# A graph network's dense part and the norm behind it as one program of five groups, and look-ups in batches of four columns

## The reference

```python
    x = x + _L0_gnn_ref(_layernorm(x, axis=-1), src, dst, edge_weight, ...)
    x = x + _L0_ffn_ref(_layernorm(x, axis=-1)[None], ...)[0]
# in _L0_gnn_ref:
        new_x = jax.ops.segment_sum(gathered, rows, num_segments=N_NODES)
        out1 = new_x @ hamilton1
        mean = jnp.mean(out1, axis=0)
        var = jnp.mean(jnp.square(out1 - mean), axis=0)
        out1 = (out1 - mean) * jax.lax.rsqrt(var + BN_EPS) * gamma + beta
        out1 = jnp.tanh(out1)
        return out1 @ hamilton2
# in _L0_ffn_ref:
            h = (x_flat @ W_gat).reshape(M, HEADS, NUM_EXPERTS)
```

## Time and profile before

| | |
|---|---|
| median of 3 runs | 3285.32 us (3279.65 to 3296.63) |
| the profiled execution | 3290.92 us |
| its span in the trace | 3289.1 us |
| from the first addition of stage 1 to the last copy into `HG` | 1016.85 to 1189.28 us, 172.4 us |

### The profile page before, as it was taken

How to read it: one execution, slowest core, us unless ns; L and a number is a source line. 1 busy time by engine, 2 the same in 40 slices (tenths; PEclk the granted TensorE clock), 3 DMA queues, 4 the chain that set the end, 5 groups by cost and what they waited for, 6 DMA issues and landing times. The chain is left out here.

```text
span 3289.1 us, 50105 instructions
## 1 busy us (share of the span) xinstructions
PE 2310.9 (70%) x10737; PEld 1726.7 (52%) x10738; DVE 1916.3 (58%) x4697; ACT 839.4 (26%) x2016; POOL 1502.0 (46%) x1250
## 2 busy tenths in 40 slices
PE   3567787777753589999536677777777756229973
PEld 2456565555542367777413455555555534229961
DVE  3756777777674333333475477777777755324437
ACT  0112122212111322223111344444444411003320
POOL 0487888888870027770200455555455500240023
PEclk8667777778775869999657899899899977569985
DMA  6666777777775024220252555555455523422233
GB/s 223 139 98 113 114 126 117 126 115 127 125 103 163 1 89 129 64 58 33 66 160 79 163 155 156 143 144 151 135 153 146 142 71 129 149 69 70 70 117 93
DMA packets 264384, 380.36 MB, mean 116 GB/s; under 512 B 36635, under 2 KB 195251, under 8 KB 264115
## 3 DMA queue, kind: packets, MB, share of 16 engines
q0 software_dynamic: 108320, 187.88, 29.0%
q1 hardware_dynamic: 134579, 151.42, 14.9%
q10 hardware_dynamic: 21344, 39.59, 3.3%
HBM read 247.23 MB, written 131.54 MB: 115 GB/s over the span
## 5 line engine op out<-in xcount | busy, mean ns | idle before, releaser
L1113 POOL DMA_INDIRECT sum_tab<-Vs,spot x416 | 703.8, 1692 | 180.4 <-issue 99.0
L2276 POOL DMA_INDIRECT KV<-kv_tab,iS x448 | 446.4, 996 | 276.3 <-DVE msg L2376 128.2
L1019 PE MATMUL psV<-XN,Bs 128*128 x832 | 314.9, 486 | 158.6 <-issue 131.1
L1019 PEld LDWEIGHTS psV<-XN,Bs 128*128 128x128 f32 x832 | 155.4, 226 | 291.2 <-issue 284.4
L2440 PE MATMUL psQ<-Qs,hotT 128*128 x904 | 264.5, 443 | 21.1 <-issue 12.7
L2451 PE MATMUL psO<-msg,hot 128*128 128x264 f32 x896 | 241.9, 416 | 13.9 <-DVE msg L2376 7.5
L1088 ACT COPY Vs<-psV 128x512 f32<-128x512 f32 x208 | 121.7, 585 | 470.2 <-DMA sum_tab<-Vs,spot 381.7
L2440 PEld LDWEIGHTS psQ<-Qs,hotT 128*128 128x128 f32 x904 | 182.1, 218 | 88.8 <-issue 59.1
L1538 POOL DMA_INDIRECT ST<-h_tab,src x192 | 184.0, 958 | 58.5 <-issue 58.5
L2305 DVE TENSOR_TENSOR KV<-KV,psQ 128x1024 f32<-128x1024 f32 x112 | 136.8, 1221 | 126.5 <-issue 88.9
L2451 PEld LDWEIGHTS psO<-msg,hot 128*128 128x128 f32 x896 | 172.0, 202 | 59.7 <-issue 22.0
(11 more groups left out here) (538 smaller groups left out, 4300.7 us busy)
## 6 DMA issues: line engine op xcount, KB each, us to landing
kb<-key_rows SPq DMA_DIRECT2D x104, 256.0 KB, 3.9
sum_tab<-zeros ACTq DMA_DIRECT2D x52, 256.0 KB, 3.1
parts<-sum_tab SPq DMA_DIRECT2D x20, 640.0 KB, 6.8
ye_tab<-Ye SPq DMA_DIRECT2D x20, 640.0 KB, 3.5
Y<-ye_tab SPq DMA_DIRECT2D x20, 640.0 KB, 9.6
disp_tab<-AE ACTq DMA_DIRECT2D x10, 896.0 KB, 5.6
lowB<-sort_tab SPq DMA_DIRECT2D x23, 384.0 KB, 6.2
xb<-disp_tab SPq DMA_DIRECT2D x68, 128.0 KB
```

The lines of the kernel that those rows point to most:

```text
L1019: ins = nc.tensor.matmul(psV[:, r % 2, x, :], Bs[:, q % 2, 2 * h + x, :], XN[:, bass.ds(t, 1), :].rearrange("p a d -> p (a d)"), start=Tru ...
L1113: pool.indirect_dma_start(out=sum_tabs[k], out_offset=bass.IndirectOffsetOnAxis(ap=spot[:, s, u:u + 1], axis=0), in_=Vs[:, j % VR, :], in_ ...
L2276: pool.indirect_dma_start(out=KV[:, s, u, :], out_offset=None, in_=kv_tab, in_offset=bass.IndirectOffsetOnAxis(ap=iS[:, s, u:u + 1], axis= ...
```

## The change

`gnn0_dense` takes over the work of the norm phase behind it, and does all of it by groups. The separate `norm_phase` call and its barrier go.

- The first product of a group is made behind the transposes of the next group, in 8 calls of 320 columns; `nx` and `NXT` have two buffers. The column statistics are taken on DVE by `bn_stats` and `bn_aggr` of each half group; ACT's squares go.
- `tt` has two buffers. The second product of group g + 2 stands behind the transposes of normalised group g and the 16-column product of group g - 1. DVE takes the row statistics behind each tile's addition.
- No engine uses a loop in registers here any more: all is written out.
- In `gat_phase` `LBN` goes from 8 to 4 and `LSL` from 2 to 4: twice as many batches of half the size, and one_hots stands in front of the second column of a batch instead of the third.

```diff
-        def gnn0_dense(H, gam, bet, first, key_out, keep, pen, cont, src):
+        def gnn0_dense(H, gam, bet, first, key_out, keep, pen, cont, src, XNT, w_dram, PN, sink):
...
+                        sp.dma_start(wp[:, :, :], w_dram.rearrange("(k p) n -> p k n", p=P)).then_inc(wp_in, 16)
                         for g in range(2, NG):
-                            sp.wait_ge(added, g - 1)
+                            sp.wait_ge(added, 3 * (g - 1))
...
+                        def add_up(g):
+                            pt, o = parts[:, g % 2, :, :, :], nx[:, g % 2, :, :]
+                            dve.wait_ge(part_in[g % 2], 16 * NTAB * (g // 2 + 1))
+                            if g >= 2:
+                                dve.wait_ge(turned, (g - 1) * GT)
+                            v.tensor_tensor(o, pt[:, 0, :, :], pt[:, 1, :, :], ALU.add).then_inc(added, 1)
+                            for k in range(2, NTAB):
+                                dve.wait_ge(added, 3 * g + k - 1)
+                                v.tensor_tensor(o, o, pt[:, k, :, :], ALU.add).then_inc(added, 1)
+                        def count_columns(g):
+                            for m in range(2):
+                                dve.wait_ge(ev1, 2 * g + m + 1)
+                                for hf in range(2):
+                                    at = g * GT * P + hf * HW
+                                    v.bn_stats(col_st[:, m, 2 * g + hf, :], O1T[:, m, at:min(at + HW, N)]).then_inc(counted, 1)
                         for g in range(NG):
...
+                            add_up(g)
                             if g:
...
+                                count_columns(g - 1)
+                        count_columns(NG - 1)
+                        dve.wait_ge(counted, 2 * NC)
                         for m in range(2):
...
+                            ins = v.bn_aggr(col_mv[:, m, :], col_st[:, m, :, :].rearrange("p n s -> p (n s)"))
+                            ins.then_inc(col_var, 1)
+                        dve.wait_ge(col_sd, 1)
                         c.seq(v.reciprocal(scl[:, :], scl[:, :]))
                         c.seq(v.tensor_tensor(scl[:, :], scl[:, :], gam[:, :], ALU.mult))
...
+                        c.seq(v.tensor_tensor(bia[:, :], col_mv[:, :, 0], scl[:, :], ALU.mult))
+                        c.seq(v.tensor_tensor(bia[:, :], bet[:, :], bia[:, :], ALU.subtract))
+                        dve.sem_inc(scaled, 1)
+                        def finish(g):
+                            for t in tiles(g):
+                                dve.wait_ge(mm2, t + 1)
+                                v.tensor_tensor(X[:, t, :], psA[:, t % 2, 0:D], X[:, t, :], ALU.add).then_inc(resid, 1)
+                                if t > g * GT:
+                                    dve.wait_ge(resid, t)
+                                    v.bn_stats(st[:, t - 1, :], X[:, t - 1, :]).then_inc(row_st, 1)
+                            dve.wait_ge(resid, (g + 1) * GT)
+                            v.bn_stats(st[:, (g + 1) * GT - 1, :], X[:, (g + 1) * GT - 1, :]).then_inc(row_st, 1)
+                            dve.wait_ge(row_st, (g + 1) * GT)
+                            for t in tiles(g):
+                                v.bn_aggr(mv[:, t, :], st[:, t, :]).then_inc(stats, 1)
+                        def evacuate(g):
+                            for t in tiles(g):
+                                dve.wait_ge(projected, t + 1)
+                                v.tensor_copy(sink[:, t, 0:PN], ps1[:, t % 2, 0:PN]).then_inc(evacuated, 1)
+                        finish(0)
+                        finish(1)
+                        for g in range(NG):
+                            dve.wait_ge(rooted, g + 1)
+                            v.reciprocal(rs[:, group(g)], sd[:, group(g)]).then_inc(inverse, 1)
+                            dve.wait_ge(inverse, g + 1)
+                            if g >= 2:
+                                dve.wait_ge(x_turned, (g - 1) * GT)
+                            for t in tiles(g):
+                                v.tensor_scalar(xn[:, g % 2, t % GT, :], X[:, t, :], mv[:, t, 0:1], rs[:, t:t + 1], ALU.subtract, ALU.mult).then_inc(normed, 1)
+                            if g:
+                                evacuate(g - 1)
+                            if g + 2 < NG:
+                                finish(g + 2)
+                        evacuate(NG - 1)
...
+                        def turn_sums(g):
+                            pe.wait_ge(added, 3 * (g + 1))
+                            for t in tiles(g):
+                                if t >= 2:
+                                    pe.wait_ge(columns, t - 1)
+                                nc.tensor.transpose(psT[:, t % 2, 0:P], nx[:, g % 2, t % GT, 0:P], ident[:, :])
+                                nc.tensor.transpose(psT[:, t % 2, P:D], nx[:, g % 2, t % GT, P:D], ident[:, :]).then_inc(turned, 1)
+                        def first_product(g):
+                            pe.wait_ge(columns, (g + 1) * GT)
+                            for m in range(2):
+                                if g:
+                                    pe.wait_ge(ev1, 2 * g + m - 1)
+                                for hf in range(2):
+                                    for k in range(2):
+                                        ins = nc.tensor.matmul((ps1, psA)[m][:, hf, 0:HW], H[0][:, k, m * P:(m + 1) * P], NXT[:, g % 2, k, hf * HW:(hf + 1) * HW],
+                                                               start=(k == 0), stop=(k == 1))
+                                ins.then_inc(mm1, 1)
+                        def second_product(g):
+                            pe.wait_ge(tanhs, g + 1)
+                            for t in tiles(g):
+                                if t >= 2:
+                                    pe.wait_ge(resid, t - 1)
+                                for k in range(2):
+                                    ins = nc.tensor.matmul(psA[:, t % 2, 0:D], tt[:, g % 2, k, t % GT * P:(t % GT + 1) * P], H[1][:, k, :], start=(k == 0), stop=(k == 1))
+                                ins.then_inc(mm2, 1)
+                        def turn_rows(g):
+                            for t in tiles(g):
+                                pe.wait_ge(normed, t + 1)
+                                if t >= 2:
+                                    pe.wait_ge(laid, t - 1)
+                                nc.tensor.transpose(psT[:, t % 2, 0:P], xn[:, g % 2, t % GT, 0:P], ident[:, :])
+                                nc.tensor.transpose(psT[:, t % 2, P:D], xn[:, g % 2, t % GT, P:D], ident[:, :]).then_inc(x_turned, 1)
+                        def project(g):
+                            for t in tiles(g):
+                                pe.wait_ge(laid, t + 1)
+                                if t >= 2:
+                                    pe.wait_ge(evacuated, t - 1)
+                                for k in range(2):
+                                    ins = nc.tensor.matmul(ps1[:, t % 2, 0:PN], XNT[:, g, k, t % GT * P:(t % GT + 1) * P], wp[:, k, :], start=(k == 0), stop=(k == 1))
+                                ins.then_inc(projected, 1)
                         keys_on_tensor(pe)
...
+                        for g in range(NG):
+                            turn_sums(g)
+                            if g:
+                                first_product(g - 1)
+                        first_product(NG - 1)
+                        second_product(0)
+                        second_product(1)
+                        pe.wait_ge(wp_in, 16)
+                        pe.wait_ge(ev1, 2 * NG)
+                        for g in range(NG):
+                            turn_rows(g)
+                            if g:
+                                project(g - 1)
+                            if g + 2 < NG:
+                                second_product(g + 2)
+                        project(NG - 1)
...
+                        def lay_sums(g):
+                            if g >= 2:
+                                act.wait_ge(mm1, 2 * (g - 1))
+                            for t in tiles(g):
+                                act.wait_ge(turned, t + 1)
+                                a.copy(NXT[:, g % 2, :, t % GT * P:(t % GT + 1) * P], psT[:, t % 2, 0:D].rearrange("p (k c) -> p k c", k=2)).then_inc(columns, 1)
+                        def keep_product(g):
                             for m in range(2):
...
+                                act.wait_ge(mm1, 2 * g + m + 1)
+                                a.copy(O1T[:, m, g * GT * P:(g + 1) * GT * P].rearrange("p (a c) -> p a c", a=2), (ps1, psA)[m][:, :, 0:HW]).then_inc(ev1, 1)
+                        def squash(g):
+                            if g >= 2:
+                                act.wait_ge(mm2, (g - 1) * GT)
                             for m in range(2):
...
```

(66 more changed lines are left out.)

71 lines of the change are left out of this document (15 added, 56 removed).

## The result

The changed kernel takes 3187.48 us (median of 4 runs, 3183.78 to 3193.24) against 3285.51 us of the kernel before in the same comparison (4 runs, 3279.65 to 3296.63): ratio 0.970, 95% interval 0.967 to 0.973. That is 98 us less, where 16 were forecast and 30 were the most that the range allowed. The prediction was wrong, and not by a shade.

The account below looks back on a forecast made before the run. The prediction took the 172.4 us changed stretch as a chain of hand-offs between engines, with no engine busy throughout. Terms of -6.3, -8.5 and -1.5 gave -16.3 us from the median 3285.32: 3269.0 us, range 3255 to 3281.

Parts of the forecast that it names:

- All of that is in the 172.4 us, so I cost the whole stretch anew: All work removed, look-ups aside, lies between the first addition and the end of the norm; only this stretch was costed anew.
- Additions and first product: First half of the changed stretch, up to the tanh: rounds of 16.3 us, tanh starting 6.3 us earlier.
- The chain: Additions, transposes, previous group's product, copy, statistics, next additions wait on each other in a closed chain: 16.3 us a round.
- the product: A group's first product, 8 calls of 320 columns on PE: 7.0 us, bounds 4.4 and 8.7.
- the 5.2 us at the low clock: Each first product after a pause begins at PE's low clock and stays there for 5.2 us.
- Copy and statistics: ACT's copy and DVE's column statistics behind each first product: 1.8 us a round, of which statistics 0.85 and copy 0.7.
- Second product and norm: Second half of the changed stretch, from the tanh's start: 81.6 us instead of 90.1, 8.5 us less.
- the two rounds: Two rounds of additions, transposes, small product and second product in the norm: 16.7 us each.
- the clock comes sooner or stays: Rival: PE's clock is high earlier in the products; 3249 if all high, 3259 for half of it; chance 0.20.
- pauses of 2.33 us: Evidence for the clock rival: in the second-product stage before, PE's pauses of 2.33 us kept its clock up.
- Table loads: ACT's four extra loads cost nothing under PE's second product; rival with them on the path: 5.1 us, 3274, chance 0.12.
- Look-ups: Four slots remove PE's wait for a batch's numbers: 1.5 us less; rival that this does nothing: 3270.5, chance 0.10.

Follow-up runs that it names:

- before_dve27: Kernel before with 27 small memsets added on DVE, putting its attention loop where the changed kernel has it: 3217.92 us, ratio 0.980.
- experiment 2: Kernel before with 50 more copies on ACT and 15 more products on TensorE: ratio 1.002; dense part alone with a DVE loop and 126 memsets: 0.975.
- dense_dve5: Kernel before with only the dense part of the change (look-ups as before) and 5 small memsets on DVE: 3197.69 us, ratio 0.973.
- open_chain: Changed kernel with a group's column statistics two additions later instead of one, on a slow chip: 3618.64 us, ratio 0.980.
- after: The changed kernel itself in the first comparison with the kernel before: 3187.48 us, ratio 0.970.
- after_c: The changed kernel unaltered, run again on a chip like the first: 3185.16 us, ratio 0.969 to the kernel before.
- open_both_c: Changed kernel with column statistics one addition later and the next group's rows normalised ahead of the last additions, chip like the first: 3167.31 us, ratio 0.964.
- after_b: The changed kernel unaltered, run again on a slow chip: 3633.56 us, ratio 0.983 to the kernel before.
- after_dve88: Changed kernel with 88 small memsets added on DVE, on a slow chip: ratio 0.992 to the kernel before.

## Why the prediction was wrong

- **The step that failed** is "All of that is in the 172.4 us, so I cost the whole stretch anew". The work is all there; the effect is not. The prediction put everything behind the look-ups at nothing, without a reason. There DVE's loop in the attention was being fetched again in each pass, and in the changed kernel it isn't: -71.3 us in the profiled execution, and -65.4 in before_dve27 with 27 idle instructions alone. The wait was in the trace of before, as 88.9 us of "issue" in front of one line of DVE; I had read only the stages around the change. Which part of the change switches it off is open (experiment 2): dense_dve5, whose loop stands where it stood before, has it off too (-61.6).
- **Additions and first product**: forecast -6.3, measured -14.7 us (1016.85 to 1099.18 before, 1012.18 to 1079.79 after). The chain was right, and open_chain shows it; the term that was mis-sized is the product: 7.0 us forecast, 4.8 to 5.7 measured. I took the 5.2 us at the low clock from one row as a fixed time, where the product had 2.3 to 0.5. Over four products that is 7.4 of the 8.4 us missed. Copy and statistics were well put (0.69 and 0.89 us for one half; the other lies under the product).
- **Second product and norm**: forecast 81.6 us, measured 74.5. Of the 7.1 us, 4.1 were gained by the end of product 2 (22.5 us after the tanh's start, 26.6 forecast; its 4.78 us are a product at the high clock, which had risen 0.5 us into it), 1.9 in the two rounds (15.5 and 16.1 for 16.7) and 1.1 at the end.
- **The clock as a rival**: "the clock comes sooner or stays" had 0.20 and 3259 in its likelier form. For the changed stretch and the look-ups alone it was the true one: 32.4 us less, where the forecast had 16.3, this rival's likelier form 26.3 and its full form 36.3. One of the rows that spoke for it was read too well: pauses of 2.33 us did not always keep the clock up. In the fourth product of that stage, which took 6.24 us, it was down again:

```profile
1126.64:1130.05 3.41, 3.41 (x10) 2.65 (x9) 1.02 (x3) 0.00 (x0) 0.00 (x0) 0.50 0.00 0
```

- **Table loads**: right, they are under PE's product. The root starts 1.29 us after its load does (1089.35 to 1090.64), again without the drain that the Trainium skill, "ScalarE: Activation LUTs", What ACT_TABLE_LOAD costs, adds to it.
- **Look-ups**: right, within what can be told: the experts' stage takes 406.2 to 406.4 us with the new look-ups (after, after_c, open_both_c) and 407.2 to 408.7 without them (seven runs on such chips); forecast 1.5 less.
- **The slower rival** (a clock that never rises) was ruled out by the first round.

The sum with measured sizes: -30.3 - 2.1 = -32 us from what was changed, and -64 (before_dve27's) from the refetch that stopped, -96 of the -98 measured.

## What to carry to other kernels

Before costing an edit, look in the whole trace for "issue" time in front of an instruction that stands in a loop, and for packets of the instruction queues there: if some stage fetches its loop again, any edit ahead of it on that engine can win or lose more than its own work, and such an edit's timing says nothing of the edit until that is held fixed (compare with a few idle instructions added). A result many times the forecast is to be placed by stages first; here two thirds of it lay in code that nobody had touched. And the time that PE's clock took to rise in one place is no constant to add up with: here it was anything from 3.3 to 10.0 us after PE's first instruction, so a term that rests on it needs bounds as wide.

## What was not expected of the hardware

- The refetch itself: some 60 packets of 8 KB, 64 to 71 us of 3285, switched by 27 idle instructions.
- The same kernel takes 3185 us on one chip and 3634 on another, and 199 us of the difference is TensorE waiting for no one in one stage. Waits of PE in the experts' stage, after_b:

```profile
PE psY L1756 <- issue: 103.9, 4, 54.2
PE psH L1745 <- issue: 94.8, 9, 66.0
```

  The stage takes 667.1 us instead of 406.4. Nearly all of these stalls lie between 1199 and 1466 us, and POOL's gathers of `ST` run from 1199.7 to 1443.7; each gather takes 952 ns at the median, as on the other chips. My expectations took it for code that comes late. The trace doesn't bear that out: between 1200 and 1460 us a single packet of TensorE's code (queue 8) arrives, and there are several long stalls. The attention too takes some 150 us more on these chips. There DVE's "issue" rises with the refetch as it does elsewhere, from 23.9 us (after_b) to 105.5 (after_dve88), but the attention only from 930.9 to 948.2: presumably DVE isn't alone in waiting. What holds TensorE there was not found.
